# A megakernel's attention block: scores of four heads in one block of products on separate rows, four decay buffers, and filler products in the gate chain

## The chip, the cores and the metric

The kernel runs on one core of a Trainium2 chip. The metric is the device time of one execution in microseconds (us), of which the median of three runs is taken. The engines are PE (TensorE), DVE (VectorE), ACT (ScalarE), POOL (GpSimd) and SP, which here only issues DMAs. Each has its own instruction stream; semaphores order them.

## The reference, cut to what matters

The program is two layers of attention and feed-forward. The change touches only the attention of the first layer. It takes the layer-normed `x` as queries and `ctx` as keys and values: 8 batches of 256 rows, 8 heads of 32 columns each.

```
log_f_cum = cumsum(log_sigmoid(fg))
log_D = where(ltr, log_f_cum[s] - log_f_cum[t] + ig[t], -inf)
D = exp(log_D - max_log_D)
qk = einsum('bhsd,bhtd->bhst', qh, kh) / sqrt(dh)          # dh = 32
C = qk * D
normalizer = maximum(abs(sum(C)), exp(-max_log_D))
h = einsum('bhst,bhtd->bhsd', C / (normalizer + 1e-6), vh)
h_norm = (h - mean) / sqrt(var + 1e-5) * norm_w            # over the 32 columns of a head
x = x + h_norm
```

Behind it follow a mixture of 32 experts, a long convolution with two small feed-forwards, and a dense mixture of 8 experts, none of them changed.

## The kernel before

There are 64 heads in all, i = 0 to 63 (batch b = i // 8, head h = i % 8). The kernel first transposes `ctx` and the normed `x` into `kT` and `qT` (32 rows per head, four heads on the 128 partitions), and forms the gates with 64 matmul passes (the products of line 1475). Then comes the gate chain: ScalarE and VectorE work out softplus, running sum and running maximum on small tiles, with two table loads, while PE waits. PE transposes the rows (line 1479), ScalarE copies them into `aT` and `eE`, and the head loop starts.

For each head the loop does this, with tokens of the keys on the partitions and only the causal part (256 + 128 columns):

- PE, `scores(i)`: two fp32 products of all 128 rows of `kT` with `qM`, a copy of the queries in which the rows of the other heads are zero (lines 1491, 1492), into PSUM bank i % 2. An fp32 product is two passes, each with a weight load of its own; the trace has them as two records. POOL makes `qM` with one copy of 32 rows per head (line 1324), twelve buffers deep.
- PE, same function: three products (lines 1496 to 1498) that add up mask and decay exponents in bank 2 + i % 2. They are bf16 and single-pass fp32.
- ACT: two exponentials from that bank to the decay rows `Dm[i % 2]` (lines 1045, 1046).
- DVE: the mix, `Cm[i % 3] = scores * Dm` (line 555).
- PE, `values(i)`: three fp32 products of 33 columns with `Cm` as weights (lines 1507 to 1509), two heads behind the scores. The 33rd column is the row sum.

Once per batch DVE also does four pieces for the batch before, placed by hand behind mixes 2, 3, 4 and 7: the normaliser (five operations on 16 elements, lines 525 to 529), the division of all 512 columns into `hN` (line 539), the mean (lines 543, 544) and the variance (lines 548, 549). POOL subtracts the mean (line 1338), ACT squares the result (line 1040), behind the exponentials of head 6.

Every engine's order is written out by hand. The waits that tie the loop: scores wait for the mix of head i - 2 (`mixed_done`), the decay products for the exponentials of head i - 2 (`decay_done`), the exponentials for the mix of head i - 2 (`Dm`), the mix for the values of head i - 3 (`Cm`).

After the loop, the last batch is normalised, ACT takes logarithm and exponential of the variance with two table loads, then a SiLU with another; PE waits for it with the products of line 1533.

## Time and profile before

| | us |
|---|---|
| median of three runs | 1977.99 |
| lowest and highest | 1974.35, 1978.93 |
| profiled execution | 1975.1 |
| its span in the trace | 1973.3 |
| head loop, first scores to end of last mix | 63.79 to 175.87 |

The span is the time from the first to the last instruction of the profiled execution; the rest lies around it. Times in the rows below are from the span's start. A row of the timeline has start, duration, engine, line, operation, output and inputs, shapes and the number of instructions merged into it; what stands in brackets is how long the engine was idle before it and what released it. Ends of matmuls are modelled, so distances between starts on PE say more than durations.

### The profile page before, as it was taken

What the parts mean: (1) busy time and instruction counts of PE and PEld (TensorE: products, weight loads), DVE (VectorE), ACT (ScalarE), POOL (GpSimd) and SP (SyncE); (2) the same over time, 40 slices, a digit from 0 to 9 for tenths busy, and PEclk for the clock granted to TensorE, in tenths of its full rate; (3) what the DMA queues carried; (4) which work ended last, traced back from release to release, by engine and by line L of the source; (5) the groups of instructions that cost most, each with busy time, mean ns of one, the idle gap of its engine ahead of it and who ended that gap; (6) DMA issues with size and microseconds to landing.
All of it is one profiled execution on the core that took longest, in us unless ns stands there. A gap on an engine that the chain in (4) does not pass through costs nothing.

```text
span 1973.3 us, 28728 instructions
## 1 busy us (share of the span) xinstructions
PE 1669.9 (85%) x9522; PEld 1434.5 (73%) x9522; DVE 1257.0 (64%) x2540; ACT 504.8 (26%) x848; POOL 473.7 (24%) x363
## 2 busy tenths in 40 slices
PE   4798534867888257759999999999999999999998
PEld 4796423425887146647888888888888888888887
DVE  4353479784566477545767676766666666767675
ACT  2444011212333245542211121212121212121121
POOL 1233324773780761000101010101010100101010
PEclk9898756987999577779999999999999999999999
DMA  9100001323775330000000000000000000000001
GB/s 367 39 1 11 17 0 40 131 70 98 241 235 156 100 96 22 1 16 17 32 16 32 16 32 16 31 17 18 30 16 32 16 32 16 32 16 32 16 0 43
DMA packets 53807, 106.00 MB, mean 54 GB/s; under 512 B 6512, under 2 KB 37808, under 8 KB 53744
## 3 DMA queue, kind: packets, MB, share of 16 engines
q1 hardware_dynamic: 21488, 63.21, 9.3%
q10 hardware_dynamic: 26112, 25.17, 4.1%
q0 software_dynamic: 6144, 16.79, 2.6%
q8 instruction: 38, 0.62, 0.1%
q14 instruction: 25, 0.20, 0.0%
HBM read 69.50 MB, written 35.65 MB: 53 GB/s over the span
## 4 chain that ended last, share of the span: by engine, by line
PE 77%; DVE 13%; ACT 3%; DMA 3%; issue 2%; SPq 1%; POOL 0%; ACTq 0%; DVEq 0%; POOLq 0%
PE ps L1598 36%; PE ps L1614 19%; PE ps L1692 3%; PE ps L1652 2%; DMA xl<-slots_in 2%; PE ps L1768 2%; PE ps L1491 2%; PE ps L1790 2%; DVE st L465 1%; PE ps L1711 1%; PE ps L1672 1%; DVE x L812 1%; PE ps L1547 1%; PE ps L1571 1%; PE ps L1492 1%
## 5 line engine op out<-in xcount | busy, mean ns | idle before, releaser
L1598 PE MATMUL ps<-xTH,wH 128*128 128x512 f32 x1024 | 401.7, 392 | 0.0
L1598 PE MATMUL ps<-xTH,wL 128*128 128x512 f32 x1024 | 401.5, 392 | 0.0
L1598 PE MATMUL ps<-xTL,wH 128*128 128x512 f32 x1024 | 398.4, 389 | 0.0
L1098 ACT ACTIVATE sg<-ps 128x512 f32<-128x512 f32 x264 | 158.1, 599 | 905.1 <-PE ps L1598 905.0
L960 DVE TENSOR_TENSOR hF<-sg,ps 128x512 f32<-128x512 f32 x256 | 175.9, 687 | 305.7 <-ACT sg L1098 305.7
L1365 POOL TENSOR_TENSOR wL<-wS,wH 128x1536 fp32r<-128x1536 f32 x32 | 112.4, 3514 | 963.0 <-ACT wH L1093 963.0
L1614 PE MATMUL ps<-wL,hH 128*128 128x256 f32 x1024 | 289.8, 283 | 0.0
L1614 PE MATMUL ps<-wH,hL 128*128 128x256 f32 x1024 | 289.7, 283 | 0.0
L1614 PE MATMUL ps<-wH,hH 128*128 128x256 f32 x1024 | 288.5, 282 | 0.5 <-DVE hL L969 0.5
L969 DVE TENSOR_TENSOR hL<-hF,hH 128x512 fp32r<-128x512 f32 x256 | 258.2, 1009 | 0.1
L979 DVE SCALAR_TENSOR_TENSOR x<-ps,cw,x 128x256 f32<-128x256 f32 x512 | 222.6, 477 | 1.0 <-PE ps L1614 1.0
L1598 PEld LDWEIGHTS ps<-xTL,wH 128*128 128x128 f32 x1024 | 192.4, 188 | 42.0
L1598 PEld LDWEIGHTS ps<-xTH,wH 128*128 128x128 f32 x1024 | 193.3, 189 | 33.6
L1598 PEld LDWEIGHTS ps<-xTH,wL 128*128 128x128 f32 x1024 | 193.3, 189 | 30.4
L1614 PEld LDWEIGHTS ps<-wH,hH 128*128 128x128 f32 x1024 | 195.5, 191 | 10.6 <-DVE hL L969 0.7
L1614 PEld LDWEIGHTS ps<-wH,hL 128*128 128x128 f32 x1024 | 195.5, 191 | 9.9
L1614 PEld LDWEIGHTS ps<-wL,hH 128*128 128x128 f32 x1024 | 195.5, 191 | 0.0
L963 DVE CAST hH<-hF 128x512 fp32r<-128x512 f32 x256 | 109.6, 428 | 39.6 <-PE ps L1614 30.2
L1393 POOL DMA_INDIRECT slots_in<-xn,idS x64 | 80.5, 1259 | 39.5 <-issue 39.5
L1692 PE MATMUL ps<-eHL,hH 128*128 x384 | 82.5, 298 | 2.3 <-DVE hL L759 2.3
L555 DVE SCALAR_TENSOR_TENSOR Cm<-ps,Dm 128x384 f32<-128x384 f32 x64 | 35.7, 557 | 57.7 <-ACT Dm L1046 54.6
L1418 POOL DMA_INDIRECT yg<-slots_out,idG x64 | 67.0, 1047 | 21.9 <-issue 19.1
(361 smaller groups left out, 2578.6 us busy)
## 6 DMA issues: line engine op xcount, KB each, us to landing
wS<-in_w SPq DMA_DIRECT2D x32, 768.0 KB, 4.4
slots_in<-qM SPq DMA_DIRECT2D x16, 768.0 KB, 14.3
eS<-in_wr SPq DMA_DIRECT2D x32, 384.0 KB, 3.8
xl<-slots_in ACTq DMA_DIRECT2D x48, 256.0 KB, 3.0
slots_out<-yo ACTq DMA_DIRECT2D x48, 256.0 KB, 3.4
x<-in_x SPq DMA_DIRECT2D x1, 2048.0 KB, 8.8
cx<-in_ctx SPq DMA_DIRECT2D x1, 2048.0 KB, 14.4
out<-x SPq DMA_DIRECT2D x4, 512.0 KB, 2.9
```

The costliest lines, as they stand in the source:

```text
L960: dve.tensor_tensor(hF[:, b, :], sg[:, b, :], ps[:, 2 + b, :], ALU.mult).then_inc(mul_done, 1)
L963: dve.tensor_copy(hH[:, b, :], hF[:, b, :]).then_inc(h_high, 1)
L969: dve.tensor_tensor(hL[:, b, :], hF[:, b, :], f32(hH[:, b, :]), ALU.subtract).then_inc(h_low, 1)
L979: dve.scalar_tensor_tensor(x[:, tile, :], acc, cw2[:, tile, bass.ds(it, 1)], x[:, tile, :], ALU.mult, ALU.add).then_inc(evac_done, 1)
L1098: act.activation(sg[:, b, :], ps[:, b, :], ACT.Silu).then_inc(silu_done, 1)
L1365: pool.tensor_tensor(blocks(wL, slot, plain), blocks(wS, slot, plain), f32(blocks(wH, slot, plain)), ALU.subtract).then_inc(w_low, 1)
L1393: pool.indirect_dma_start(xs_d, bass.IndirectOffsetOnAxis(ap=idS[:, n, k:k + 1], axis=0), xn[:, n, :], None, bounds_check=TILES * P - 1, o ...
L1418: pool.indirect_dma_start(yg[:, n % 4, k, :], None, ys_d, bass.IndirectOffsetOnAxis(ap=idG[:, n, k:k + 1], axis=0), bounds_check=TILES * P ...
L1491: pe.matmul(ps[:, i % 2, 0:256], kT[:, c, t0:t0 + P], qM[:, i % 12, :], start=True, stop=True)
L1598: last = pe.matmul(ps[:, 2 * half + b, :], piece(w, s, slot, col, P), v[:, k, g * 512:(g + 1) * 512], start=q == 0, stop=q == 5)
L1614: last = pe.matmul(o, h[:, b, t * P:(t + 1) * P], piece(w, s, slot, col, D), start=(opens and t % 2 == 0 and q == 0), stop=(closes and q = ...
L1692: last = pe.matmul(ps[:, 2 + b, t * D:(t + 1) * D], h[:, b, (2 * t + k) * P:(2 * t + k + 1) * P], eFlat[:, bass.ds(off + (w + k * D), D)], ...
```

## The change

1. Scores of four heads at once. `scores(i)` now runs once per four heads. Each head's two products take only its own 32 rows of `kT` and of `qT` (no masked copy), and go to banks 0 to 3. All 256-column products come first, then the 128-column ones. The group waits for the last mix of the group before. The 64 masking copies on POOL are gone.
2. The decay products become a function of their own, on banks 4 and 5. `Dm` and `Cm` have four buffers each. The exponentials wait for the mix of head i - 4, the mix for the values of head i - 4.
3. The values of a batch go to one bank per half (heads 0 to 3 in bank 6, 4 to 7 in bank 7), so the normaliser and the division run per half: behind mix 6 for the first half, behind mix 2 of the next batch for the second. Mean and variance stay behind mixes 4 and 7.
4. PE issues 42 products of `idb` with `maskT` (384 columns, bf16) behind the gate products, and ten more behind the two transposes. Nobody reads them.

```diff
-        Dm = at("Dm", [P, 2, 384], F32, end["cx"])
-        Cm = at("Cm", [P, 3, 384], F32, end["Dm"])
+        Dm = at("Dm", [P, 4, 384], F32, end["cx"])
+        Cm = at("Cm", [P, 4, 384], F32, end["Dm"])
...
+            def half_out(b, half):
+
+                hs = slice(4 * half, 4 * half + 4)
+                o = ps[:, 6 + half, 0:8 * (DH + 1)].rearrange("p (s h d) -> p s h d", s=2, h=4)
+                v = hN[:, b % 2, :].rearrange("p (s h d) -> p s h d", s=2, h=NH)[:, :, hs, :]
+                dn = den[:, :, hs]
+                dve.wait_ge(pv_done, 8 * b + 4 * half + 4)
+                link(dve.tensor_copy(dn, o[:, :, :, DH]))
+                link(dve.scalar_tensor_tensor(dn, dn, -1.0, dn, ALU.mult, ALU.max))
+                link(dve.tensor_tensor(dn, dn, eE[:, :, 8 * b + 4 * half:8 * b + 4 * half + 4], ALU.max))
+                link(dve.tensor_scalar(dn, dn, 1e-6, None, ALU.add))
+                link(dve.reciprocal(dn, dn))
+                wait(dve, head_centred, b - 1)
+                dve.tensor_tensor(v, o[:, :, :, 0:DH], dn.unsqueeze(3).to_broadcast([P, 2, 4, DH]), ALU.mult).then_inc(head_read, 1)
...
             for i in range(B * NH):
                 dve.wait_ge(qk_done, i + 1)
                 dve.wait_ge(decay_done, i + 1)
-                wait(dve, pv_done, i - 2)
-                dve.scalar_tensor_tensor(Cm[:, i % 3, :], ps[:, i % 2, 0:384], float(DH) ** -0.5, Dm[:, i % 2, :],
+                wait(dve, pv_done, i - 3)
+                dve.scalar_tensor_tensor(Cm[:, i % 4, :], ps[:, i % 4, 0:384], float(DH) ** -0.5, Dm[:, i % 4, :],
                                          ALU.mult, ALU.mult).then_inc(mixed_done, 1)
-                if i >= 8 and i % 8 in (2, 3, 4, 7):
-                    head_work(i // 8 - 1, (2, 3, 4, 7).index(i % 8))
-            for part in range(4):
-                head_work(B - 1, part)
+                if i % 8 == 6:
+                    half_out(i // 8, 0)
+                if i >= 8 and i % 8 == 2:
+                    half_out(i // 8 - 1, 1)
+                if i >= 8 and i % 8 == 4:
+                    head_mean(i // 8 - 1)
+                if i >= 8 and i % 8 == 7:
+                    head_variance(i // 8 - 1)
+            half_out(B - 1, 1)
+            head_mean(B - 1)
+            head_variance(B - 1)
...
-                wait(act, mixed_done, i - 1)
-                act.activation(Dm[:, i % 2, 0:256], ps[:, 2 + i % 2, 0:256], ACT.Exp, bias=aT[:, 0, i:i + 1])
-                act.activation(Dm[:, i % 2, 256:384], ps[:, 2 + i % 2, 256:384], ACT.Exp, bias=aT[:, 1, i:i + 1]).then_inc(decay_done, 1)
+                wait(act, mixed_done, i - 3)
+                act.activation(Dm[:, i % 4, 0:256], ps[:, 4 + i % 2, 0:256], ACT.Exp, bias=aT[:, 0, i:i + 1])
+                act.activation(Dm[:, i % 4, 256:384], ps[:, 4 + i % 2, 256:384], ACT.Exp, bias=aT[:, 1, i:i + 1]).then_inc(decay_done, 1)
...
-            def mask_queries(heads):
-                for i in heads:
-                    if i < B * NH:
-                        r, c, t0 = DH * (i % 4), i % NH // 4, i // NH * SEQ
-                        wait(pool, qk_done, i - 11)
-                        pool.tensor_copy(qM[r:r + DH, i % 12, :], qT[r:r + DH, c, t0:t0 + SEQ]).then_inc(q_masked, 1)
-                        pool.wait_ge(q_masked, i + 1)
...
+            def spare(bank, count):
+
+                for _ in range(count):
+                    pe.matmul(ps[:, bank, 0:384], idb[:, :], maskT[:, :], start=True, stop=True)
...
+            pe.wait_ge(id2_done, 1)
+            spare(6, 42)
             pe.wait_ge(rows_done, 1)
             for h in range(2):
                 last = pe.transpose(ps[:, 5, h * P:(h + 1) * P], AE[:, h * P:(h + 1) * P], ident[:, :])
             last.then_inc(rowsT_done, 1)
+            spare(6, 10)
...
             def scores(i):
-                b, h = i // NH, i % NH
-                c = h // 4
+                b, c = i // NH, i % NH // 4
                 t0 = b * SEQ
-                wait(pe, mixed_done, i - 1)
-                pe.wait_ge(q_masked, i + 1)
-                pe.matmul(ps[:, i % 2, 0:256], kT[:, c, t0:t0 + P], qM[:, i % 12, :], start=True, stop=True)
-                pe.matmul(ps[:, i % 2, 256:384], kT[:, c, t0 + P:t0 + SEQ], qM[:, i % 12, P:],
-                          start=True, stop=True).then_inc(qk_done, 1)
+                wait(pe, mixed_done, i)
+                for part in range(2):
+                    first = part * P
+                    for j in range(4):
+                        r = DH * j
+                        last = pe.matmul(ps[:, j, 2 * first:2 * first + SEQ - first], kT[r:r + DH, c, t0 + first:t0 + first + P],
+                                         qT[r:r + DH, c, t0 + first:t0 + SEQ], start=True, stop=True)
+                last.then_inc(qk_done, 4)
+
+            def decays(i):
                 wait(pe, decay_done, i - 1)
-
-                pe.matmul(ps[:, 2 + i % 2, 0:384], idb[:, :], maskT[:, :], start=True, stop=False, skip_group_check=True)
-                pe.matmul(ps[:, 2 + i % 2, 0:256], sel[:, i, :], MHL[:, :], start=False, stop=False, skip_group_check=True)
-                pe.matmul(ps[:, 2 + i % 2, 256:384], sel[:, i, :], MHL[:, P:SEQ], start=False, stop=True,
+                pe.matmul(ps[:, 4 + i % 2, 0:384], idb[:, :], maskT[:, :], start=True, stop=False, skip_group_check=True)
+                pe.matmul(ps[:, 4 + i % 2, 0:256], sel[:, i, :], MHL[:, :], start=False, stop=False, skip_group_check=True)
+                pe.matmul(ps[:, 4 + i % 2, 256:384], sel[:, i, :], MHL[:, P:SEQ], start=False, stop=True,
                           skip_group_check=True).then_inc(arg_done, 1)
 
             def values(i):
                 b, h = i // NH, i % NH
-                o0, o1 = (ps[:, 4 + 2 * (b % 2) + s, h * (DH + 1):(h + 1) * (DH + 1)] for s in range(2))
+                o0, o1 = (ps[:, 6 + h // 4, (4 * s + h % 4) * (DH + 1):(4 * s + h % 4 + 1) * (DH + 1)] for s in range(2))
                 pe.wait_ge(mixed_done, i + 1)
-                if h == 0:
-                    wait(pe, head_read, b - 1)
-                pe.matmul(o0, Cm[:, i % 3, 0:P], vext[:, 2 * b, h, :], start=True, stop=True)
-                pe.matmul(o1, Cm[:, i % 3, P:2 * P], vext[:, 2 * b, h, :], start=True, stop=False)
-                pe.matmul(o1, Cm[:, i % 3, 2 * P:3 * P], vext[:, 2 * b + 1, h, :], start=False, stop=True).then_inc(pv_done, 1)
-
-            for i in range(B * NH):
+                if h % 4 == 0:
+                    wait(pe, head_read, i // 4 - 1)
+                pe.matmul(o0, Cm[:, i % 4, 0:P], vext[:, 2 * b, h, :], start=True, stop=True)
+                pe.matmul(o1, Cm[:, i % 4, P:2 * P], vext[:, 2 * b, h, :], start=True, stop=False)
+                pe.matmul(o1, Cm[:, i % 4, 2 * P:3 * P], vext[:, 2 * b + 1, h, :], start=False, stop=True).then_inc(pv_done, 1)
+
+            decays(0)
+            decays(1)
+            for i in range(0, B * NH, 4):
                 scores(i)
-                if i >= 2:
-                    values(i - 2)
-            values(B * NH - 2)
+                if i:
+                    values(i - 1)
+                decays(i + 2)
+                decays(i + 3)
+                values(i)
+                if i + 4 < B * NH:
+                    decays(i + 4)
+                values(i + 1)
+                if i + 4 < B * NH:
+                    decays(i + 5)
+                values(i + 2)
             values(B * NH - 1)
```

PE, in the middle of the head loop. `scores` are the products with `kT`, the decay block those with `maskT` and `MHL`, `values` those with `Cm`. Before, one head:

```order
L1491 MATMUL ps<-qM,kT 128x256
L1492 MATMUL ps<-qM,kT 128x128
L1496 MATMUL ps<-maskT,idb 128x384
L1497 MATMUL ps<-MHL,sel 128x256
L1498 MATMUL ps<-MHL,sel 128x128
L1507 MATMUL ps<-vext,Cm 128x33
L1508 MATMUL ps<-vext,Cm 128x33
L1509 MATMUL ps<-vext,Cm 128x33
```

The same place in the changed kernel, where a group of four heads starts:

```order
L1497 MATMUL ps<-qT,kT 128x256 x4
L1497 MATMUL ps<-qT,kT 128x128 x4
L1514 MATMUL ps<-vext,Cm 128x33
L1515 MATMUL ps<-vext,Cm 128x33
L1516 MATMUL ps<-vext,Cm 128x33
L1503 MATMUL ps<-maskT,idb 128x384
L1504 MATMUL ps<-MHL,sel 128x256
L1505 MATMUL ps<-MHL,sel 128x128
```

Eight score products stand in a row, and the values and decay blocks of the four heads follow behind them, one by one.

DVE, one batch of the head loop, from mix 0. Before:

```order
L555 SCALAR_TENSOR_TENSOR Cm<-ps,Dm 128x384 x3
L525 COPY den<-ps 128x16
...
L529 RECIPROCAL den<-den 128x16
L555 SCALAR_TENSOR_TENSOR Cm<-ps,Dm 128x384
L539 TENSOR_TENSOR hN<-ps,den 128x512
L555 SCALAR_TENSOR_TENSOR Cm<-ps,Dm 128x384
L543 TENSOR_REDUCE mean<-hN 128x16
L544 TENSOR_SCALAR mean<-mean 128x16
L555 SCALAR_TENSOR_TENSOR Cm<-ps,Dm 128x384 x3
L548 TENSOR_REDUCE var<-hQ 128x16
```

The same batch in the changed kernel, from mix 0 to mix 7:

```order
L554 SCALAR_TENSOR_TENSOR Cm<-ps,Dm 128x384 x3
L528 COPY den<-ps 128x2x4
...
L534 TENSOR_TENSOR hN<-ps,den 128x2x128
L554 SCALAR_TENSOR_TENSOR Cm<-ps,Dm 128x384 x2
L540 TENSOR_REDUCE mean<-hN 128x16
L541 TENSOR_SCALAR mean<-mean 128x16
L554 SCALAR_TENSOR_TENSOR Cm<-ps,Dm 128x384 x2
L528 COPY den<-ps 128x2x4
...
L534 TENSOR_TENSOR hN<-ps,den 128x2x128
L554 SCALAR_TENSOR_TENSOR Cm<-ps,Dm 128x384
```

The five normaliser operations and a division now stand twice in a batch, both times whole between two mixes, and one of them just ahead of mix 7.

PE, between the gate products and the head loop, in the changed kernel:

```order
L1459 MATMUL ps<-maskT,idb 128x384 x42
L1482 MATMUL ps<-ident,AE 128x128 x2
L1459 MATMUL ps<-maskT,idb 128x384 x10
L1503 MATMUL ps<-maskT,idb 128x384
L1504 MATMUL ps<-MHL,sel 128x256
L1505 MATMUL ps<-MHL,sel 128x128
```

Before, only the two transposes stood there, and the loop began with the scores of head 0; now it begins with the decay blocks of heads 0 and 1.

## Rows read from the trace of the kernel before

**Rows 1.** The page: busy time of PE, its share of the span

```profile
PE 1669.9 (85%) x9522; PEld 1434.5 (73%) x9522; DVE 1257.0 (64%) x2540; ACT 504.8 (26%) x848; POOL 473.7 (24%) x363
```

**Rows 2.** Windows: stretch, length; busy PE, PEld, DVE, ACT, POOL; PEclk; DMA

```profile
71.00:89.00 18.00, 18.00 (x140) 17.36 (x138) 7.90 (x18) 7.50 (x21) 1.18 (x3) 1.00 0.01 1
```

**Rows 3.** Timeline, PE, one head of the loop and the next one's start

```profile
123.53 0.68 PE L1491 MATMUL ps<-qM,kT 128*128 128x256 f32 x2
...
124.04 0.38 PE L1492 MATMUL ps<-qM,kT 128*128 128x128 f32 x2
...
124.26 0.33 PE L1496 MATMUL ps<-maskT,idb 128*128 128x384 bf16 x1
...
124.60 0.36 PE L1507 MATMUL ps<-vext,Cm 128*128 128x33 f32 x2
...
125.24 0.68 PE L1491 MATMUL ps<-qM,kT 128*128 128x256 f32 x2
```

**Rows 4.** Timeline, PE behind the loop

```profile
188.27 2.08 PE L1533 MATMUL ps<-Wp,h1T 128*128 128x256 f32 x4 [7.85 <-ACT h1T L1062]
```

**Rows 5.** Timeline, PE, gate products of 256 columns, fp32

```profile
38.88 1.03 PE L1475 MATMUL ps<-kT,gateW 128*128 128x256 f32 x4
39.74 1.03 PE L1475 MATMUL ps<-qT,gateW 128*128 128x256 f32 x4
```

**Rows 6.** Timeline, the same head's exponentials and mix

```profile
124.80 0.47 ACT L1045 ACTIVATE Dm<-ps,aT 128x256 f32<-128x256 f32 x1 [0.98 <-PE ps L1498]
...
125.62 0.56 DVE L555 SCALAR_TENSOR_TENSOR Cm<-ps,Dm 128x384 f32<-128x384 f32 x1 [1.16 <-ACT Dm L1046]
```

**Rows 7.** Timeline, the pieces of a batch on DVE, POOL and ACT

```profile
120.49 0.56 DVE L555 SCALAR_TENSOR_TENSOR Cm<-ps,Dm 128x384 f32<-128x384 f32 x1 [1.16 <-ACT Dm L1046]
...
120.96 0.68 DVE L548 TENSOR_REDUCE var<-hQ 128x16 f32<-128x512 f32 x1
...
126.10 0.17 DVE L525 COPY den<-ps 128x16 f32<-128x16 f32 x1
...
126.92 0.25 DVE L529 RECIPROCAL den<-den 128x16 f32<-128x16 f32 x1
...
127.92 0.68 DVE L539 TENSOR_TENSOR hN<-ps,den 128x512 f32<-128x512 f32 x1
...
129.53 0.68 DVE L543 TENSOR_REDUCE mean<-hN 128x16 f32<-128x512 f32 x1
...
130.56 1.05 POOL L1338 TENSOR_TENSOR hC<-hN,mean 128x512 f32<-128x512 f32 x1 [9.01 <-DVE mean L544]
...
132.28 0.63 ACT L1040 ACTIVATE hQ<-hC 128x512 f32<-128x512 f32 x1
```

**Rows 8.** Timeline, the last mix and those who waited for it

```profile
175.31 0.56 DVE L555 SCALAR_TENSOR_TENSOR Cm<-ps,Dm 128x384 f32<-128x384 f32 x1 [1.16 <-ACT Dm L1046]
...
175.92 0.41 PE L1507 MATMUL ps<-vext,Cm 128*128 128x33 f32 x2 [0.16 <-DVE Cm L555]
...
176.82 0.17 DVE L525 COPY den<-ps 128x16 f32<-128x16 f32 x1
```

**Rows 9.** Groups of instructions, 420 to 900 us: a 128x256 product on DVE

```profile
L764 DVE TENSOR_TENSOR rh<-rs__162,ps 128x256 f32<-128x256 f32 x48 | 20.2, 421 | 23.0 <-ACT rs__162 L1157 22.9
```

**Rows 10.** Windows around the gate chain and the loop's start

```profile
56.00:58.00 2.00, 0.00 (x0) 0.00 (x0) 1.49 (x3) 0.41 (x1) 0.00 (x0) 0.50 1.07 304
...
69.00:70.00 1.00, 1.00 (x9) 0.94 (x7) 0.50 (x1) 0.03 (x1) 0.39 (x1) 0.70 0.00 0
```

**Rows 11.** Timeline, PE, row transposes, first scores, fourth scores

```profile
60.96 0.69 PE L1479 MATMUL ps<-ident,AE 128*128 128x128 f32 x2 [8.96 <-DVE MHL L520]
...
63.79 1.19 PE L1491 MATMUL ps<-qM,kT 128*128 128x256 f32 x2 [2.15 <-ACT eE L1034]
...
70.41 0.68 PE L1491 MATMUL ps<-qM,kT 128*128 128x256 f32 x2
```

**Rows 12.** Windows, a stretch of the convolution

```profile
362.00:378.00 16.00, 11.37 (x30) 4.07 (x28) 9.31 (x11) 5.55 (x3) 12.65 (x12) 1.00 0.61 212
```

More of the change, by code:

```diff
@@ L256, in build @@
         rowsT_copied = sem("rowsT_copied")
-        q_masked = sem("q_masked")
         qk_done = sem("qk_done")
@@ L520, in _ @@
             dve.tensor_copy(MHL[64:, :], r2[0:64, :]).then_inc(rows_done, 1)
-            def head_normaliser(b, o):
-                dve.wait_ge(pv_done, 8 * (b + 1))
-                link(dve.tensor_copy(den[:, :, :], o[:, :, :, DH]))
-                link(dve.scalar_tensor_tensor(den[:, :, :], den[:, :, :], -1.0, den[:, :, :], ALU.mult, ALU.max))
-                link(dve.tensor_tensor(den[:, :, :], den[:, :, :], eE[:, :, 8 * b:8 * b + 8], ALU.max))
-                link(dve.tensor_scalar(den[:, :, :], den[:, :, :], 1e-6, None, ALU.add))
-                link(dve.reciprocal(den[:, :, :], den[:, :, :]))
@@ L531, in head_work @@
-            def head_work(b, part):
-                o = ps[:, 4 + 2 * (b % 2):6 + 2 * (b % 2), 0:NH * (DH + 1)].rearrange("p s (h d) -> p s h d", h=NH)
-                v = hN[:, b % 2, :].rearrange("p (s h d) -> p s h d", s=2, h=NH)
-                if part == 0:
-                    head_normaliser(b, o)
-                if part == 1:
-                    wait(dve, head_centred, b - 1)
-                    dve.tensor_tensor(v, o[:, :, :, 0:DH], den[:, :, :].unsqueeze(3).to_broadcast([P, 2, NH, DH]),
-                                      ALU.mult).then_inc(head_read, 1)
-                if part == 2:
-                    dve.wait_ge(head_read, b + 1)
-                    link(dve.tensor_reduce(mean[:, b % 2, :, :], v, AXX, ALU.add))
-                    dve.tensor_scalar(mean[:, b % 2, :, :], mean[:, b % 2, :, :], 1.0 / DH, None, ALU.mult).then_inc(head_scaled, 1)
-                if part == 3:
-                    dve.wait_ge(head_squared, b + 1)
-                    q = hQ[:, b % 2, :].rearrange("p (s h d) -> p s h d", s=2, h=NH)
-                    link(dve.tensor_reduce(var[:, b, :, :], q, AXX, ALU.add))
-                    dve.tensor_scalar(var[:, b, :, :], var[:, b, :, :], 1.0 / DH, EPS, ALU.mult, ALU.add).then_inc(head_var, 1)
@@ new lines, in head_mean, with head_variance @@
+            def head_mean(b):
+                v = hN[:, b % 2, :].rearrange("p (s h d) -> p s h d", s=2, h=NH)
+                dve.wait_ge(head_read, 2 * b + 2)
+                link(dve.tensor_reduce(mean[:, b % 2, :, :], v, AXX, ALU.add))
+                dve.tensor_scalar(mean[:, b % 2, :, :], mean[:, b % 2, :, :], 1.0 / DH, None, ALU.mult).then_inc(head_scaled, 1)
+            def head_variance(b):
+                dve.wait_ge(head_squared, b + 1)
+                q = hQ[:, b % 2, :].rearrange("p (s h d) -> p s h d", s=2, h=NH)
+                link(dve.tensor_reduce(var[:, b, :, :], q, AXX, ALU.add))
+                dve.tensor_scalar(var[:, b, :, :], var[:, b, :, :], 1.0 / DH, EPS, ALU.mult, ALU.add).then_inc(head_var, 1)
@@ L1331, in rows_of @@
                 return ap.rearrange("p s h -> p (s h)").unsqueeze(2).to_broadcast([P, 2 * NH, DH])
-            mask_queries(range(10))
             for b in range(B):
-                mask_queries(range(8 * b + 10, 8 * b + 18))
                 hc = hC[:, b, :].rearrange("p (g d) -> p g d", d=DH)
@@ L1526, in _ @@
             pe.wait_ge(pos1_silu, 1)
-            pe.wait_ge(head_read, B)
+            pe.wait_ge(head_read, 2 * B)
             for lt in range(4):
```

## The prediction, as it was put on record

> **What bounds the kernel now.** I read the page first: TensorE is busy 85% of the span, VectorE 64% [rows 1]. The change touches only the first attention block, so I then read its stretch, from 63.8 us (first score product) to 175.9 us (end of the last mix of scores and decay). In it PE is busy every microsecond at full clock and VectorE and ScalarE about half the time [rows 2]; the same holds in each window from 71 to 161 us. The timeline shows why: per head PE issues scores (0.51 + 0.22 us), the three decay products (0.34) and the three value products (0.64), and the next head starts 1.71 us after the last one [rows 3]. Sixty-four heads at 1.71 are 109.7 of the 112.1 us. So the loop is bound by PE's own issue; every wait of the two other engines is for PE. What follows it is a serial chain (normalise, two table loads, SiLU) and PE waits for its end [rows 4], so a gain before it arrives one for one, and nothing later hangs on the wall clock.
>
> **PE's work.** Values: six passes (two for each fp32 product) in 0.64 us, so 0.107 us a pass for only 33 columns: that is the price of loading 128 weight columns, since the streams are tiny [rows 3]. A 256-column pass costs 0.215: four in 0.86 in the gate products [rows 5]. So a 128-column pass streams for 0.107.
> Now four heads' scores are sixteen passes, each over its own 32 rows (eight of 256 columns, eight of 128). Before they took 4 x 0.73 = 2.92 us. Call the new block S. No row shows products on different rows at once, so I bound it. Upper end: no overlap at all, 8 x 0.215 + 8 x 0.107 = 2.58. Lower end: four row groups stream truly side by side, 2 x 0.215 + 2 x 0.107 = 0.65. Between: if products start in order, the second pass of a head must wait for its first on the same rows, while the next head's first pass may join it; the 256-column part becomes five steps of 0.215 and the 128-column part three more steps of 0.107, 1.40 us. And if weight loads don't overlap each other, sixteen of them at 0.107 are 1.71, plus 0.05 for the first start: 1.76. I take S = 1.76, since the nearest row, the value products, is bound by just that load.
> The Trainium skill ("TensorE: Matmul & The Clock Gate", LDWEIGHTS) says that a load costs by its columns and that 32 rows take as long as 128. The 0.107 us of the rows agrees for 128 rows; nothing here shows 32. The same page (Part 3, measured speedup) gives 3.07x for four row tiles of 512 columns: by it S would be 0.84.
>
> **The new loop.** PE work per four heads falls from 6.85 to S + 4 x 0.98 = 5.7 us. But that is no longer the bound. The scores of a group overwrite all four banks, so they wait for the last mix of the group before, and that mix waits for what stands on VectorE ahead of it. I follow the chain with durations of before. A decay block's start to its exponentials 0.54, these to the mix 0.82 [rows 3, 6]. A mix gives way to the next after 0.47 and is done after 0.56 (120.49, 120.96) [rows 7]. PE starts 0.05 after a mix ends (175.31 + 0.56, 175.92), and VectorE reads a last product 0.27 after PE is free of it (0.64 after 175.92 is 176.56; the next reader starts at 176.82) [rows 8]. A half normaliser: the five small operations 1.07 plus 0.03, and the product over half the columns, 0.42 as the nearest 128x256 row has it [rows 9]: 1.55 with gaps. It now runs twice per batch of eight heads, 3.1 us against 1.07 + 0.68 once. The mean takes 0.88 (129.53 to 130.56, less the hand-off to POOL), the variance has the same shapes, the centring on POOL 1.05 [rows 7].
> First group of a batch: S, then values of the head before 0.63, decay to exponential 0.54, exponential to third mix 0.82, 0.47, half normaliser 1.55, fourth mix 0.56, 0.06 to PE: S + 4.63 = 6.39 us.
> Second group: S + 0.27, first mix 0.47, mean 0.88, POOL 0.1 + 1.05, square 0.58, exponentials of the fourth head 0.79 (they stand behind the square on ScalarE, which waits for POOL), the decay block that needs their bank 0.35, values of the third head 0.63: S + 5.1 = 6.86 us. The chain through the second half normaliser ends some 0.3 us sooner.
> A batch: 13.25 us against 8 x 1.713 = 13.70. The loop thus gains only 0.45 us a batch: PE is freed of 1.16 us per group, and most of that turns into waiting. Worked through from the first decay block (two blocks now come before any scores): first batch 12.3 (no old batch to normalise), six at 13.25, the last until its last mix 12.9, in all 104.7 us.
>
> **The gate chain.** Before, PE idles from 52.0 to 60.96 [rows 11], and the granted clock, 1.00 up to 56, is 0.50 from there (1.2 instead of 2.4 GHz) and comes back only between 69 and 70 [rows 10]. The fourth head's scores start at 70.41. From 63.79 that is 6.62 us, for three heads of scores and decay (1.07 each) and one values block (0.64), 3.85 at full clock: the fall costs 2.8 us. The change fills the wait with 42 products of 384 bf16 columns. The decay block has 768 columns in 0.34 us, so one costs 0.17: 7.1 us, ending at 59.1, 1.8 us before the transposes are released, and ten more end by 63.2, before the exponential table is there. They delay nothing and should keep the clock. At 1.2 GHz they would take 14.3 us and push the transposes from 60.96 to 66.3, but the clock is 1.00 at their start.
>
> **Sum.** Before: 63.79 to 175.87 = 112.1. After: 104.7. Gain 7.4 (of it 2.8 by the clock, 3.2 by seven batches, the rest at the ends), plus 0.24 for transposes at full clock, plus 0.27 for the half-width product of the tail: 7.9, say 8.0 us. The 64 mask copies of POOL, 0.39 us each, vanish; PE waited for none, so they count nothing. Two more buffers and the changed banks cost nothing by themselves. The profiled execution took 1975.1 (span 1973.3), so its like would take 1967.1. The three timed runs have the median 1977.99; I go half-way between, from 1976.6, to 1968.6.
>
> **Rivals.**
> (a) Scores overlap in steps, S = 1.40. Sixteen groups gain 0.36 each, 5.8 more: 1962.8. For it: loads of different rows need not share anything. Against: the value rows.
> (b) Nearly full overlap, S = 0.84, the skill's ratio: from the bounds it lies just above 0.65, and gains 14.7 more, 1953.9 (1951 at 0.65). Against it: two passes per head on the same rows.
> (c) Slower: the row groups don't overlap at all. S = 2.58 adds 16 x 0.82 = 13.1, so 1981.7, since the group's wait stands where free-running double buffers stood. The point from which this decides is S = 2.26 us; above it the change loses. This is also the case in which the change doesn't do what its words say.
> (d) Dearer hand-offs. The chain has about nine hand-offs a group, where the old loop had none on its path; 0.05 us more for each is 7.2 us: 1975.8, no change. The skill ("TensorEngine Tiling (Array Packing)", Key Properties) adds that a change of tiling mode drains the engine; there are 32 such changes, and no row prices one. At 0.05 to 0.15 us each, which is my guess between nothing and one load, 1.6 to 4.8 us would go the same way.
> (e) The clock falls inside the loop. PE now idles about 1.9 of 13.25 us. Against it: from 362 to 378 us PE is busy 11.37 of 16 us and the clock stays at 1.00 [rows 12]. At 1.2 GHz PE's own 11.4 us a batch would double: over 70 us slower.
>
> **How the numbers follow.** My forecast 0.35, (a) 0.22, (b) 0.08, (c) 0.15, (d) 0.15, (e) 0.05. A measurement here can tell about 0.2%, 4 us. Faster by more: 0.35 + 0.30 + a third of (d) = 0.70. Slower: (c) and most of (e), 0.18. Within: 0.12. The range reaches from (b), 1953, to just past (c), 1982; outside are (e) and the far end of (b).
>
> **What would show it.** The score line's block: sixteen passes in 1.76 us, or 1.4, or 2.6. A batch of 13.25 us from one group of scores to the second next. VectorE waiting for PE at the first mix of a group, PE waiting for the mix before each group of scores, for about 0.5 us or more. The clock 1.00 from 50 to 177 us. The first scores near 64.2, the last mix ending near 168. If the batch is longer though S is right, my hand-offs were too cheap; if the stretch after the attention loop changes by over 2 us, the gain isn't passed on as I say.

## The result and the profile of the changed kernel

The changed kernel takes 1999.52 us (median of four runs, 1996.23 to 2002.18), the kernel before beside it 1976.95. The ratio is 1.0114 (95% interval 1.0091 to 1.0137): 22.6 us slower, where I had forecast 8 to 9 us faster. In a later session the same kernel had 1.0112 (1.0098 to 1.0125). The profiled execution took 1996.23 us.

The page of the changed kernel: its span, the busy times (beside [rows 1]), and the granted clock in 40 slices of 49.9 us each.

```profile
span 1994.4 us, 28710 instructions
...
PE 1694.7 (85%) x9574; PEld 1453.9 (73%) x9574; DVE 1260.2 (63%) x2588; ACT 502.5 (25%) x848; POOL 445.8 (22%) x299
...
PEclk9855656986999667788999999999999999999999
```

TensorE's busy time went up, although the change removes work from it. Slices 3 and 4, counted from 1, are 100 to 200 us, the attention loop, and the clock digit there is 5. Windows of the changed kernel give it by stage (columns as in [rows 2]; the eighth number is the granted clock):

```profile
52.00:64.00 12.00, 9.44 (x58) 5.46 (x57) 4.61 (x11) 6.12 (x9) 0.00 (x0) 1.00 0.49 154
64.00:80.00 16.00, 15.31 (x160) 14.51 (x163) 8.62 (x24) 9.79 (x28) 0.00 (x0) 1.00 0.01 3
80.00:87.00 7.00, 6.12 (x72) 5.69 (x66) 5.19 (x15) 3.33 (x9) 1.05 (x1) 1.00 0.00 0
...
100.00:120.00 20.00, 20.00 (x112) 19.12 (x112) 9.46 (x28) 6.94 (x19) 1.05 (x1) 0.50 0.00 1
...
200.00:220.00 20.00, 14.25 (x26) 6.68 (x24) 0.93 (x3) 7.03 (x12) 15.66 (x14) 0.50 0.00 0
```

The gate chain and the first 23 us of the loop run at the full 2.4 GHz. At about 87 us the clock falls to 0.50 (1.2 GHz), and it is 0.50 for the rest of the loop and beyond. There PE is busy every microsecond, with half as many instructions in the same time. The timeline of PE shows the groups (`scores` is line 1497, its decay blocks line 1503, the fillers line 1459; columns as in [rows 3]):

```profile
61.35 0.44 PE L1482 MATMUL ps<-ident,AE 128*128 128x128 f32 x2 [2.15 <-DVE MHL L519]
...
64.61 0.94 PE L1497 MATMUL ps<-qT,kT 32*128 32x256 f32 x16
65.47 0.34 PE L1503 MATMUL ps<-maskT,idb 128*128 128x384 bf16 x1
...
74.34 0.94 PE L1497 MATMUL ps<-qT,kT 32*128 32x256 f32 x16 [0.35 <-DVE Cm L554]
79.70 0.94 PE L1497 MATMUL ps<-qT,kT 32*128 32x256 f32 x16 [0.34 <-DVE Cm L554]
84.62 0.34 PE L1503 MATMUL ps<-maskT,idb 128*128 128x384 bf16 x1 [0.88 <-ACT Dm L1052]
...
85.39 0.39 PE L1516 MATMUL ps<-vext,Cm 128*128 128x33 f32 x2
85.71 0.94 PE L1497 MATMUL ps<-qT,kT 32*128 32x256 f32 x16
93.71 1.67 PE L1497 MATMUL ps<-qT,kT 32*128 32x256 f32 x16
102.99 1.66 PE L1497 MATMUL ps<-qT,kT 32*128 32x256 f32 x16
```

The sixteen passes take 65.47 - 64.61 = 0.86 us. At full clock a batch of two groups takes 85.71 - 74.34 = 11.37 us against 13.70 before, and PE waits for the last mix of a group as foreseen (0.35, 0.34). It waits longest, 0.88 us, ahead of a decay block in the second group of a batch: the block needs a bank that ScalarE's exponentials must read first, and these stand behind the square. At half clock a group takes 9.28 us (93.71 to 102.99), a batch 18.56, and the brackets with the waits are gone: PE's own issue is the bound. The instructions of line 554, the mixes, show where the loop ends (duration min/median/max in ns, first and last start), and whom DVE waited for:

```profile
L554 DVE SCALAR_TENSOR_TENSOR Cm<-ps,Dm x64: 545/557/559, 65.6 to 192.9; 128x384 f32<-128x384 f32 x64
...
  PE ps L1497: 49.4, 16
```

The account against before: the last mix ends at 193.5 instead of 175.9, which is 17.6 us; behind it 1800.9 us are left instead of 1797.4, another 3.5. Together 21.1, the difference of the spans.

### The profile page after: what moved, and what is told of

Its sections match the earlier page's. It is cut to its first block, busy times and chain, and to the rows that moved or that the text cites. A ratio compares the mean times of both kernels' runs of the same rounds, so it can differ in the third digit from the quotient of the medians.

```text
span 1994.4 us, 28710 instructions
## 1 busy us (share of the span) xinstructions
PE 1694.7 (85%) x9574; PEld 1453.9 (73%) x9574; DVE 1260.2 (63%) x2588; ACT 502.5 (25%) x848; POOL 445.8 (22%) x299
## 4 chain that ended last, share of the span: by engine, by line
PE 77%; DVE 13%; ACT 3%; DMA 3%; issue 2%; SPq 1%; POOL 0%; DVEq 0%; ACTq 0%; POOLq 0%
PE ps L1615 36%; PE ps L1631 19%; PE ps L1709 3%; PE ps L1669 2%; DMA xl<-slots_in 2%; PE ps L1785 2%; PE ps L1807 2%; DVE st L464 1%; PE ps L1728 1%; PE ps L1516 1%; PE ps L1514 1%; PE ps L1515 1%; PE ps L1497 1%; PE ps L1689 1%; PE ps L1503 1%
```

## Experiments

Each ratio is to the kernel before on the same chip, in the same session. "Held" means that the mean granted clock of an execution was 0.915 to 0.922, about as before (0.913 to 0.918); where the clock of a grouped loop fell for long, or was low from its start, it was 0.882 to 0.905. Only one execution of each run has a trace; for the others the mean clock and the time are all that tells.

### Does the clock decide, and can it be held?

If the clock fell because PE has less to do, unread full-height products ahead of each group's scores should hold it. One edit, with k = 8 and k = 3:

```diff
             for i in range(0, B * NH, 4):
+                if i:
+                    spare(0, k)
                 scores(i)
```

> The changed kernel with eight unread products of 384 bf16 columns (about 0.16 us each) on bank 0 ahead of the scores of each group but the first. Theory A (the granted clock follows how much of the time the array streams columns; four heads' scores now stream in 0.87 us what took 2.9, so the loop streams too little to hold or regain full clock): 15 x 1.3 us of streaming come back, the clock stays 1.00 from 50 us to the end of the loop, a batch of eight heads takes 11.4 us plus at most 2 x 0.9 (0.4 of each block lies in the idle time ahead of the scores), 13.2, and the kernel takes about 1965 us, at least 8 below before. Theory B (products on 32 rows as such bring the clock down): clock 0.50 from about 87 us, a batch 18.6 plus 2 x 2.6, over 2035 us.

> The same with three unread products ahead of each group: about the 0.35 to 0.46 us that PE idles there, nothing more. Theory C (the idle stretches ahead of the groups bring the clock down): the clock holds 1.00, a batch takes 11.5 us, the kernel about 1957 us. Theory A: only 0.5 us of streaming per group comes back where 2 us went; I expect the fall to 0.50 somewhere in the loop, and then about 2000 us or a little more.

With eight: 1975.37 us (ten executions), ratio 0.9986 (0.9971 to 1.0000), the clock held in all ten. PE does more per group and the kernel is 24 us faster than the changed one. Against before it gains nothing: a batch takes 13.53 us (88.22 to 101.75, from one of the long waits to the next), where 13.2 was expected and the old loop had 13.70. With three: one execution, 1960.48, held, with a batch of 11.93 us (74.72 to 86.65). So the clock, not the schedule, makes the loss. But three are a thin margin:

> The changed kernel with three unread full-height products ahead of each group but the first, timed. One execution gave 1960.5 us. If three products (0.5 us of 128-row streaming a group) are enough to hold the clock every time, the median is 1958 to 1963 us and the spread about that of the kernel before. If the margin is thin, some executions fall to 0.50 in the loop as the changed kernel does and the times spread from 1957 to over 2000.

Six more executions: 1964.31 and 1964.98 held; the other four took 1995.61 to 2013.13 us at a mean clock of 0.887 to 0.897. The same code either stays at full clock or falls.

### Is it the height of the products?

The changed loop differs from the old one in timing too. Here is the kernel before, its order and waits untouched, with only the scores taken from the head's own 32 rows (the masked copies are still made and waited for):

```diff
-                pe.matmul(ps[:, i % 2, 0:256], kT[:, c, t0:t0 + P], qM[:, i % 12, :], start=True, stop=True)
+                r = DH * (i % 4)
+                pe.matmul(ps[:, i % 2, 0:256], kT[r:r + DH, c, t0:t0 + P], qT[r:r + DH, c, t0:t0 + SEQ], start=True, stop=True)
```

and so for the 128-column product.

> The kernel before, with each head's scores taken from its own 32 rows of the queries and keys instead of 128 rows with a masked copy (the copies are still made and waited for). The order, the count and the columns of all products are as before. Theory A with streaming time as the measure: nothing changes, 1.71 us a head, clock 1.00 from 70 us on, 1977 us. Theory B: the clock falls or never comes up in the loop, a head takes 2.3 to 2.7 us and the kernel over 2015 us.

2094.77 us (one execution), 117 us slower, for the same number of products of the same columns. Its window and one head of its timeline:

```profile
80.00:100.00 20.00, 20.00 (x77) 17.29 (x75) 2.79 (x5) 4.25 (x12) 0.39 (x1) 0.50 0.00 1
...
121.85 1.22 PE L1492 MATMUL ps<-qT,kT 32*128 32x256 f32 x2
122.86 0.63 PE L1493 MATMUL ps<-qT,kT 32*128 32x128 f32 x2
123.43 0.50 PE L1497 MATMUL ps<-maskT,idb 128*128 128x384 bf16 x1
...
125.40 1.22 PE L1492 MATMUL ps<-qT,kT 32*128 32x256 f32 x2
```

A head takes 3.55 us instead of 1.71. The change of rows has a price of its own here: from the start of the 128-column scores to the decay block it is 0.57 us, and 0.42 at the same half clock in the kernel before (64.78 to 65.20), and the next scores start 0.11 us late as well. That is about 0.25 us a head; the rest is the clock. Before, the loop begins at half clock too and raises it within 6 us [rows 10]; with 32-row scores it never does. The rows that went carried only the zeros of the masked copy. To see whether they would at least keep a clock that is full at the start, the 52 gate fillers of the change were added to this kernel:

> The kernel before with each head's scores from its own 32 rows and with the 52 unread products of the gate chain, so that the loop starts at full clock. Theory D, the loop streams too little over many rows even to hold the clock: it falls within some 30 us of the loop's start and stays at 0.50, a head then takes 3.5 us instead of 1.71, about 2080 us. If the 32-row loop can hold a clock and only can't raise it: 1.00 all through, 1974 us.

2165.36 us (one execution) against 2050.64 for the kernel before. On this chip that one too was 72 us longer; in each of the three traces from it ScalarE waits 55 to 56 us at one place of the convolution, and why isn't known, so only runs of this chip are compared with each other. The window:

```profile
60.00:80.00 20.00, 19.16 (x79) 15.77 (x80) 3.35 (x7) 6.24 (x15) 2.37 (x6) 0.63 0.00 1
```

The first scores start at 62.64 at full clock; it falls at 65.2, after two heads, and is 0.50 for the rest of the loop. The fall itself doesn't prove that 32-row products can't keep a clock, since PE had waited 2.15 and 0.52 us just before the loop. In one of the two traces of the old loop with the gate fillers (below) the clock falls at 61.3, too, but there the 128-row products have it back at 64.8. What the two runs with 32-row scores show is that their loop doesn't raise the clock.

The same question for the fillers: eight of them, as long as before, over 32 rows.

```diff
-                    pe.matmul(ps[:, bank, 0:384], idb[:, :], maskT[:, :], start=True, stop=True)
+                    pe.matmul(ps[:, bank, 0:384], idb[0:DH, :], maskT[0:DH, :], start=True, stop=True)
```

> The changed kernel with eight unread products ahead of each group as in the version with eight that held the clock (same type, same 384 columns), but over 32 rows instead of 128. Theory D (the clock answers to streaming over many rows; products on 32 rows count for little however long they stream): the clock falls in the loop as in the changed kernel, a group takes 9.3 us plus up to 8 x 0.32 at half clock, 2020 to 2045 us. If only the streaming time counts: as the version with 128 rows, clock 1.00, 1975 us.

2004.96 us (one execution), less than the 2020 to 2045 expected, because the clock held until 126.7 us and fell only then; with eight full-height ones it held in all ten, and in twelve more further down. The windows of this kernel, and below of the eight full-height ones:

```profile
120.00:140.00 20.00, 19.12 (x124) 16.52 (x124) 8.53 (x25) 6.41 (x18) 1.05 (x1) 0.67 0.00 1
140.00:160.00 20.00, 20.00 (x108) 17.46 (x106) 7.82 (x24) 5.19 (x15) 1.05 (x1) 0.50 0.00 0
```

```profile
140.00:160.00 20.00, 18.29 (x175) 15.52 (x175) 12.27 (x37) 9.00 (x26) 2.06 (x2) 1.00 0.01 1
```

Before its fall, from 80 to 100 us, the 32-row one had PE busy 18.23 of 20 us: the busy share doesn't tell them apart. PE changes between 32-row and 128-row products equally often in both, so the number of changes isn't the cause either. A product of 32 rows differs from a full one in its height and in using one of four row groups; which of these counts isn't separated, for no kernel here has products of 64 rows.

And the other way round: the groups, buffers and order of the change, but with the scores over all 128 rows from the masked copies, which POOL makes again:

```diff
-                        last = pe.matmul(ps[:, j, 2 * first:2 * first + SEQ - first], kT[r:r + DH, c, t0 + first:t0 + first + P],
-                                         qT[r:r + DH, c, t0 + first:t0 + SEQ], start=True, stop=True)
+                        last = pe.matmul(ps[:, j, 2 * first:2 * first + SEQ - first], kT[:, c, t0 + first:t0 + first + P],
+                                         qM[:, (i + j) % 12, first:SEQ], start=True, stop=True)
```

> The changed kernel with its groups, buffers and waits, but the eight score products of a group taken over all 128 rows from masked copies, as in the kernel before. Theory D: the clock stays 1.00 through the loop; the score block takes 2.6 us instead of 0.87, a batch 11.4 + 2 x 1.75 = 14.9 us, and the kernel 1980 to 1990 us, faster than the changed kernel although its products are slower. If the grouping and its waits are what brings the clock down: 0.50 in the loop, over 2015 us.

1998.58 us (one execution), above the 1980 to 1990 expected. Its clock was full but for four dips of some 3.4 us in the loop, which begin at 106.7, 123.8, 154.5 and 171.6 us; the mean clock, 0.915, doesn't show them. What the run shows besides is the price of the schedule without the overlap. Timeline of PE:

```profile
91.87 2.87 PE L1509 MATMUL ps<-qM,kT 128*128 128x256 f32 x16
94.58 0.31 PE L1526 MATMUL ps<-vext,Cm 128*128 128x33 f32 x2
...
106.84 4.49 PE L1509 MATMUL ps<-qM,kT 128*128 128x256 f32 x16
...
153.88 0.34 PE L1515 MATMUL ps<-maskT,idb 128*128 128x384 bf16 x1 [1.02 <-ACT Dm L1053]
```

Sixteen full-height passes take 94.58 - 91.87 = 2.71 us, a batch 14.97, more than the old loop's 13.70. So the groups pay only because products on different rows overlap (0.86 against 2.71). The last row stands ahead of the third dip: a wait of 1.02 us ends at 153.88, and the clock falls 0.6 us later.

### What do the gate fillers bring?

The changed kernel without its 52 gate fillers (both `spare(6, ...)` calls removed), and the kernel before with them, in two sessions:

> The changed kernel without the 52 unread products of the gate chain. The clock is then 0.50 when the loop starts. Theory A: the loop can't bring it up, 16 groups at 9.3 us, 148 us for the loop instead of 129, about 2017 us. If the loop could hold a clock but was only unlucky once, it comes up within 10 us as in the kernel before and the loop takes about 95 us, 1963 us.

> The kernel before with the 52 unread products of the gate chain alone. All theories: clock 1.00 through the gate chain and from the loop's first product; the fourth head's scores start 3.9 us after the first instead of 6.6; the kernel gains 2.8 us in the loop plus 0.2 at the transposes, 3.0 us or 0.15%: 1974.8 against 1977.8. If the clock falls anyway, nothing.

> The kernel before with the 52 unread products of the gate chain alone, again. All theories: 0.9982 before, so 3 to 4 us gained, in every execution, since the loop of 128-row products holds the clock by itself: ratio 0.998 to 0.9985.

Without them 2015.35 us (one execution, 2017 expected): the loop starts at half clock and never leaves it, so its mixes go from 66.1 to 208.7. Window of this kernel:

```profile
66.00:80.00 14.00, 14.00 (x79) 13.56 (x76) 5.38 (x14) 4.99 (x14) 0.00 (x0) 0.50 0.01 1
```

The old kernel with them: 1974.35 and 1974.77, ratios 0.9982 (0.9969 to 0.9995) and 0.9983 (0.9972 to 0.9993), twelve executions each. The mixes run from 65.9 to 173.1 instead of 67.0 to 175.3, and the products behind the loop [rows 4] start 2.2 us earlier. It is the one part of the change that pays by itself, although the fillers don't always keep the clock ahead of the loop: in five of the seventeen traces with them it dips to 0.50 for some 3.5 us from about 61 us on.

### How many fillers, and where?

Five and six ahead of each group:

> The changed kernel with five unread full-height products ahead of each group but the first. Three cost 0.27 us a group over none and held the clock in some executions, eight cost 1.08 us and held it in all ten. By theory D five, costing about 0.6 us a group (a batch 12.6 us), give 1965 to 1969 us where the clock holds; if it holds in all executions, the kernel is 10 us faster than before and 30 faster than the changed one. If the margin is still thin, some executions lie above 1990.

> The same with six: a batch about 12.9 us, 1967 to 1972 us where the clock holds, and fewer executions above 1990 than with five, by theory D. If the falls have nothing to do with the amount of full-height streaming, as many as with three.

Both on the chip with the stall (before: 2050.64). Their mean clocks are lower as a whole there, 0.896 to 0.902 where it held and 0.881 to 0.892 where I call it fallen. Five: 2044.16, 0.9957 (0.9939 to 0.9976), but two of twelve executions fell (2074.67, 2080.3); the ratio is of the other ten. Six: 2047.15, 0.9994 (0.9967 to 1.0021), with about four of twelve fallen wholly or in part, of which the ratio leaves out only the slowest. I read no difference between five and six into this. Then six in three places, beside eight in one and the changed kernel itself:

```diff
+                if i:
+                    spare(0, 2)
                 scores(i)
...
                 values(i)
+                spare(0, 2)
...
                 values(i + 1)
+                spare(0, 2)
```

> The changed kernel with six unread full-height products of 384 columns a group, as many as in the version with six, but two behind the values of a group's first head, two behind those of its second and two ahead of the next scores. If a weak stretch inside a group (the values are 33 columns wide) starts the falls, spreading them holds the clock in all executions, about 2% to 3% of them lost at most; the critical chain carries four of the six, so a batch takes about 13.0 us, 6 to 8 us less than before in total (ratio 0.996). If only the amount counts, or if chance decides, falls in several of 12 executions as with six in one place.

> The version with eight ahead of each group, on another occasion and beside the others. If the amount decides, no execution with a fall again (10 of 10 held) and a ratio of 0.998 to 0.999. If ten of ten was chance or a matter of the chip, some executions are 15 us or more above the others, as with five and six.

> The changed kernel itself, timed beside the others. Four executions had a mean clock of 0.891 to 0.894, so all had fallen early in the loop. Theory D: again all of them fall, 1.0% to 1.8% over the kernel before; none is faster than the kernel before. If the fall is a matter of luck, one in ten or so holds and lies near 0.99.

Spread six: 1963.21, ratio 0.9922 (0.9910 to 0.9935). Eight in one place: 1975.97, 0.9985 (0.9975 to 0.9995), twelve of twelve held. The changed kernel: 2001.62, all five fallen. The spread one's rows, a window and a batch of its timeline:

```profile
140.00:160.00 20.00, 19.52 (x189) 16.98 (x187) 13.79 (x44) 9.73 (x27) 2.10 (x2) 1.00 0.01 2
...
75.52 0.94 PE L1497 MATMUL ps<-qT,kT 32*128 32x256 f32 x16
...
86.36 0.34 PE L1503 MATMUL ps<-maskT,idb 128*128 128x384 bf16 x1 [0.23 <-ACT Dm L1052]
...
87.77 0.94 PE L1497 MATMUL ps<-qT,kT 32*128 32x256 f32 x16
```

A batch takes 12.25 us, 0.88 more than without fillers: six of 0.17 us in each of two groups are 2.0, so more than half lies in time in which PE would wait. Is it the place, or the chip? Both once more, on the chip of the spread run:

> The version with six unread products a group in three places, again, now beside the one with six in one place on the same chip. If the place decides: every execution holds the clock, ratio 0.991 to 0.993. If five of five was luck: one execution or more 15 us above the others.

> The version with six in one place, again, beside the spread one. If the place decides: several executions of it fall again for part of the loop, and those that hold lie near 0.994. If the chip decided the last time: all hold, ratio 0.993 to 0.996, and the spread version is as good.

Spread: 1965.54, 0.9943 (0.9928 to 0.9957), again all five held. Six in one place: five of eight held (1970.38 to 1974.50), three fell (1992.53 to 1996.52). The trace is of a fallen one:

```profile
120.00:140.00 20.00, 20.00 (x98) 17.04 (x97) 7.43 (x23) 6.20 (x17) 1.05 (x1) 0.50 0.00 1
```

The same amount of filler holds the clock in one arrangement and not reliably in the other; even the held ones are 6 us slower (median 1971.49), since six in a row delay the scores, for which DVE waits.

What the places differ in can be read from the traces. Six traces of grouped loops have falls inside the loop, thirteen in all: one each in the two of the changed kernel and in that with eight 32-row fillers, three each in the two with six in one place, four with full-height scores. Each begins 0.5 to 1.4 us, in one case 2.6, after the same event, the longest wait of PE in a batch, 0.85 to 1.02 us ahead of a decay block for ScalarE's exponentials. Fillers ahead of the scores leave that wait as it is. The spread ones stand just ahead of it and leave 0.23 us (86.36 above), then 0.20. The wait alone doesn't bring a fall, for with eight full-height fillers it is 0.85 to 0.88 us, too, and the clock held 22 times. No run puts fillers at that place alone, so that it is this wait which made the difference is likely, not shown.

### A loss behind the loop

Part of the 3.5 us behind the loop stands at one place. After the last product of the convolution ScalarE's queue issues the first load of the expert stage (`xl`). In the trace of before, and then of the changed kernel:

```profile
463.63 0.45 ACTq L1143 DMA_DIRECT2D xl<-slots_in  x1
```

```profile
480.63 3.22 ACTq L1149 DMA_DIRECT2D xl<-slots_in  x1
...
q14 instruction: 1, 0.01, 0.3%
```

The last row is from the queue table of the 7 us around that issue: one packet of instructions arrives on queue 14, which the window around it before doesn't have. The issue takes 0.45 us in all five traces with the old loop, without the packet, and 2.9 to 3.9 in all fourteen with the new one, with it. If it is a matter of where ScalarE's instructions lie, two waits more in its loop should move it. The spread kernel with two waits that are always met already:

```diff
+                if i in (2, 3):
+                    act.wait_ge(arg_done, i + 1)
                 wait(act, mixed_done, i - 3)
```

> The version with six unread products a group in three places, with two redundant waits on ScalarE (ahead of the exponentials of heads 2 and 3, for a semaphore already reached), which restore the number of waits that ScalarE's program had in the kernel before. Behind the convolution the first DMA issue on ScalarE's queue took 0.45 us in all five traces with the old head loop and 2.9 to 3.9 us in all eight with the new one. If the place of that issue in ScalarE's code causes it, the issue takes 0.45 us again and the kernel gains about 2.8 us over the same without the waits, ratio near 0.991. If the cause lies elsewhere (another engine's code, the timing), it stays at 3.2 us, ratio 0.993.

```profile
448.52 0.45 ACTq L1151 DMA_DIRECT2D xl<-slots_in  x1
...
452.58 1.98 PE L1695 MATMUL ps<-ident,xl 128*128 128x128 f32 x8 [4.26 <-DMA xl<-slots_in]
```

The issue is back at 0.45 us, no instruction packet is there, and PE waits 4.26 us for the load instead of 6.55 (the spread kernel's first trace). The time, 1963.33 (0.9916, 0.9899 to 0.9933, six executions), isn't told apart from 1963.21 and 1965.54 without the waits: the expert stage behind it varies by several microseconds between executions. The delay thus goes with one load of instructions, and the length of ScalarE's code decides whether it falls on this critical place; that the packet holds ScalarE's own instructions is inferred from this edit. Its worth in the total stays open between 0 and some 3 us. The Trainium skill ("DMA: Bandwidth & Descriptors", Queues, rings and completion order) lists queue row 14 as the runtime's own, refill among its uses, which agrees.

## Why the prediction was wrong, point by point

**The bound before** was read rightly: PE's own issue, and a gain or loss ahead of the products behind the loop is passed on. What came was a loss, 17.6 us in the loop, and it was passed on in full, with another 3.5 behind it. That is more than the 2 us that I allowed there; some 2.8 of it stand at ScalarE's first load of the expert stage, which I did not foresee.

**S, the score block.** I took 1.76 us, since sixteen weight loads of 0.107 us would not overlap. It is 0.86, rival (b). Sixteen full-height passes in the same order take 2.71. A weight load of 32 rows isn't shorter in the trace (184 ns on average from 64 to 86 us, 191 for full-height scores), so loads of different rows do overlap. The nearest row, the value products, ran over all 128 rows one after the other and said nothing on this; the two bounds, 0.65 and 2.58, held. The Trainium skill's 3.07x for four row tiles ("TensorE: Matmul & The Clock Gate", Part 3) was nearer: by the old block's bound it is 2.58 / 0.86 = 3.0 here, fp32 and with shorter streams.

**The chain of the new loop** was right. With S = 0.86 in place of 1.76 my two groups give 13.25 - 1.80 = 11.45 us a batch; measured while the clock was full: 11.37. Hand-offs were priced rightly, so rival (d) did not happen as a loss. The drain that it names is there, though: the scores start 0.32 us after the last value product (85.39 to 85.71), where a decay block follows such a product after 0.22 (75.67 to 75.89). At full clock a change of rows thus costs about 0.10 us, the middle of my guess of 0.05 to 0.15, and mostly it lies in the wait ahead of the scores or within the 0.86.

**Rival (c)** was no overlap. The overlap was there; but the kernel with full-height scores has a batch of 14.97 us where (c) would make it 14.9, so its price was right.

**The gate chain.** Right in the profiled execution: the clock stays 1.00 from 52 us into the loop, and the row transposes take 0.44 instead of 0.69 us. In the kernel before it is worth 3.4 to 4.2 us of median, where I had said 2.8 + 0.24. Not foreseen: in the changed kernel it is worth about 16 us (2015.35, one execution, against 1999.52 in another session), since its loop cannot raise the clock at all.

**The step that failed** is the dismissal of rival (e), the clock inside the loop, at 0.05: the clock fell to 0.50 at 87 us, and a batch took 18.56 us instead of 11.37. I argued from PE's busy share: it would idle 1.9 of 13.25 us, while a stretch of the convolution keeps 1.00 at 11.37 busy of 16 [rows 12]. Those products were full-height. The loop's score products were too, and the change turned them into 32-row ones. The experiments that change the rows and nothing else show that this matters by itself: the old loop with 32-row scores (at 0.50 throughout, PE 20.00 busy of 20), the same with full clock at its start (lost after 2.6 us and not regained in the loop), and eight fillers of 32 rows against eight of 128 (fallen in one execution, held in 22 of 22). The busy share was the wrong witness on both sides: 32-row products count as busy in the profile, and at half clock the share rises to 20 of 20.

Even so the change didn't have to fall at once: it ran at full clock for 23 us of the loop, and three fillers tip it either way. The kernel stands near an edge. The idle time that I named in (e) plays a part as well: with full-height scores in the new order the clock dips four times, and all thirteen falls follow the one long wait of a batch. How much height and how much idle time each weigh isn't separated by these runs.

**The size of (e).** I wrote over 70 us: PE's 11.4 us a batch doubled. With the true S it is 2 x 9.28 = 18.56 against 13.70 before, and nearly the first two batches still ran at full clock: the loop lost 17.6 us. The sign would have been right, the size four times too large, because S entered it, too, and because I let no batch run before the fall.

**The range** (1953 to 1982) left (e) out on purpose, and it was what happened. The chance of 0.18 for slower came nearly all from (c), so it wasn't a chance for the right reason.

**What the gain would be.** With the clock held, the single executions with three fillers show 1960 to 1965 us. The best kernel that holds it each time (16 executions in three sessions, the two extra waits in six of them) is the change with six spread fillers: medians of 1963 to 1966 us, ratios 0.9916 to 0.9943, some 12 to 15 us faster than before and 38 faster than the changed kernel beside it.

## What to carry to other kernels

Before you take full-height products off TensorE, or replace them by products on few rows, ask what holds its clock in that stretch, and don't take the busy share for the answer: look at the granted clock after the change. If it falls, unread full-height products in the places where PE waits anyway are cheap (0.17 us each here), and three pairs of them held better than six in a row; look first for the longest wait, behind which the clock falls. A wait of PE ahead of a loop that cannot raise the clock itself is worth filling most of all (about 16 us here, 4 where the loop could).

## What the runs showed of the hardware that I had not expected

- Fp32 products on four separate row groups overlap, weight loads included: sixteen passes in 0.86 us, against 2.71 over all rows. A change between 32-row and 128-row products costs about 0.10 us at full clock and 0.11 to 0.15 at half.
- Two loops with the same products in the same order, one with 32-row scores and one with 128-row ones, have a granted clock of 0.50 and 1.00, and 3.55 us a head against 1.71.
- Thirteen of thirteen falls of the clock inside the grouped loops begin within 2.6 us behind the longest wait of a batch, 0.85 to 1.02 us. In the three traces in which it is only 0.20 to 0.23 there is no fall.
- Near the edge the clock is decided anew in each execution: 1964 or 2013 us for the same kernel on the same chip.
- A load of instructions can hold up one DMA issue by 2.8 us far behind the code that was changed, and two idle waits move it away.
